# Where the embedding gathers of a DLRM tower are issued: one paced by single waits, one in bursts

## What is computed

```python
e = stack([tbl_f[ids[:, f]] for f in range(26)], axis=1)      # 2048 x 26 x 128
T = concatenate([r_dense[:, None, :], e], axis=1)             # 2048 x 27 x 128
Z = einsum('bnd,bmd->bnm', T, T)
h = concatenate([Z[:, iu0, iu1], r_dense], axis=1)            # 351 + 128 columns
h = maximum(h @ W_top1 + b_top1, 0)                           # 512
h = maximum(h @ W_top2 + b_top2, 0)                           # 256
y = h @ W_top3                                                # 2048 x 1
```

## Time and profile before

| what | us |
|---|---|
| median of 3 runs | 453.94 |
| lowest, highest | 452.58, 459.67 |
| the profiled execution | 448.83 |
| its span | 447.0 |
| TensorE busy (matmul) | 388.3 (87%) |
| VectorE busy | 262.2 (59%) |
| ScalarE busy | 156.7 (35%) |
| GpSimd busy | 235.8 (53%) |
| mean granted TensorE clock, share of 2.4 GHz | 0.950 |

### The profile page before, as it was taken

How to read it: one execution, slowest core, us unless ns; L and a number is a source line. 1 busy time by engine, 2 the same in 40 slices (tenths; PEclk the granted TensorE clock), 3 DMA queues, 4 the chain that set the end, 5 groups by cost and what they waited for, 6 DMA issues and landing times.

```text
span 447.0 us, 9767 instructions
## 1 busy us (share of the span) xinstructions
PE 388.3 (87%) x4139; PEld 353.5 (79%) x4139; DVE 262.2 (59%) x440; ACT 156.7 (35%) x215; POOL 235.8 (53%) x252
## 2 busy tenths in 40 slices
PE   7678487798988999889997999889997999898997
PEld 5568487687868889779887989779886889787897
DVE  4369558677736764666846674586845674572131
ACT  5236424251441615215351414325251424315321
POOL 6658555545655546645565456555565546556000
PEclk9869978998999999989999899999999999899899
DMA  8974211345231521234121531235121431242230
GB/s 210 252 213 125 56 47 45 96 99 166 55 85 41 140 73 41 72 90 125 37 85 42 121 92 41 84 70 148 39 67 48 105 109 48 54 108 75 41 52 18
DMA packets 48393, 39.26 MB, mean 88 GB/s; under 512 B 33073, under 2 KB 42592, under 8 KB 48350
## 3 DMA queue, kind: packets, MB, share of 16 engines
q1 hardware_dynamic: 38913, 22.38, 19.4%
q0 software_dynamic: 7808, 16.01, 14.1%
q10 hardware_dynamic: 1628, 0.25, 0.4%
HBM read 32.59 MB, written 6.03 MB: 86 GB/s over the span
## 4 chain that ended last, share of the span: by engine, by line
PE 78%; issue 10%; DVE 5%; another core or an unknown queue 3%; ACT 3%; DVEq 0%; ACTq 0%
PE look_ps L896 34%; PE gram_ps L928 15%; PE mlp_ps L948 9%; PE look_ps L906 6%; PE mlp_ps L958 5%; DVE hot L574 4%; PE look_ps L887 3%; ACT T L752 1%; ACT T L744 1%; PE look_ps L1000 1%; ACT tab_hi L719 1%; PE look_ps L970 1%; PE look_ps L992 1%; DVE hot L579 1%
## 5 line engine op out<-in xcount | busy, mean ns | idle before, releaser
L536 POOL DMA_INDIRECT rows<-in_tbl_dram,ids_all x228 | 219.2, 961 | 168.7 <-PE look_ps L896 58.3
L574 DVE TENSOR_TENSOR hot<-ids_near,gram_ps 125x2048 fp32r<-125x2048 f16 x60 | 135.7, 2285 | 77.0 <-PE look_ps L896 68.5
L896 PE MATMUL look_ps<-hot,tab_hi 125*128 125x256 f32 x664 | 172.2, 297 | 9.3 <-issue 4.2
L896 PE MATMUL look_ps<-hot,tab_lo 125*128 125x256 f32 x664 | 166.8, 289 | 0.0
L896 PEld LDWEIGHTS look_ps<-hot,tab_hi 125*128 125x128 f32 x664 | 131.5, 198 | 13.6 <-issue 7.5
L896 PEld LDWEIGHTS look_ps<-hot,tab_lo 125*128 125x128 f32 x664 | 131.7, 198 | 0.1
L744 ACT COPY T<-look_ps 128x512 f32<-128x512 f32 x38 | 45.4, 1196 | 205.2 <-PE look_ps L896 76.9
L928 PE MATMUL gram_ps<-T 128*54 128x54 f32 x2048 | 78.0, 222 | 37.3 <-issue 29.6
L928 PEld LDWEIGHTS gram_ps<-T 128*54 128x54 f32 x2048 | 66.3, 136 | 50.9 <-issue 43.0
L752 ACT COPY T<-look_ps 128x384 f32<-128x384 f32 (+2 forms) x80 | 75.7, 1050 | 34.3 <-PE look_ps L906 19.8
L606 DVE COPY gram<-gram_ps 128x486 f32<-128x486 f32 (+1 forms) x64 | 37.9, 606 | 40.4 <-remote 30.0
(11 more groups left out here) (81 smaller groups left out, 162.6 us busy)
## 6 DMA issues: line engine op xcount, KB each, us to landing
dots<-gram SPq DMA_DIRECT2D x28, 182.2 KB
ids_near<-ids_rows SPq DMA_DIRECT2D x25, 192.0 KB
rows<-in_tbl_dram,ids_all POOLq DMA_INDIRECT x228
T<-in_tbl_dram SPq DMA_DIRECT2D x4, 448.0 KB
pairs<-dots SPq DMA_DIRECT2D x14, 117.0 KB
gram<-in_tbl_dram SPq DMA_DIRECT2D x3, 448.0 KB
rows<-in_r_dense_dram SPq DMA_DIRECT2D x16, 64.0 KB
w<-in_tbl_dram SPq DMA_DIRECT2D x2, 448.0 KB
```

The source lines that it names most:

```text
L536: pool.indirect_dma_start(rows[:, t % 2, place[n], :], None, tables[n - 1], bass.IndirectOffsetOnAxis(ap=index[:, n - 1:n].bitcast(U32), a ...
L574: eq = nc.vector.tensor_tensor(hot[:VP, count % 2], near, steps[:VP].rearrange("p (c q) -> p c q", q=1).to_broadcast([VP, CH, Q]), ALU.is_ ...
L896: mm = pe.matmul(dst, w[:VP, k, c], hot[:VP, slot, c], start=(c == 0 and half == 0), stop=(c == CH - 1 and half == 1))
```

## The change

It replaces the single waits by a few: for tiles 0 to 3 EARLY names the gathers that wait, and for what. For the others BURSTS (and BURSTS_END in unit 6) says which of a unit's 30 gathers wait for which step; all others follow without a wait for pace. The waits for `turned` in gather stay. In steady state the bursts have 7, 6, 3, 5, 6 and 3 gathers.

```diff
-            STEP_MORE = (4, 5, 6, 6, 8, 8, 8, 10, 10, 11, 12, 12, 13, 13, 15, 16, 16, 17, 18, 19, 20, 21, 21, 22, 23, 23, 24, 25, 26, 26, 27, 28)
-            STEP_LESS = (4, 5, 6, 6, 8, 8, 8, 10, 10, 11, 12, 12, 13, 15, 16, 16, 17, 18, 19, 20, 21, 21, 22, 23, 24, 25, 26, 27, 28, 29)
+
+            EARLY = ({7: (hot_looked, 1), 12: (hot_looked, 3)},
+                     {0: (hot_looked, 5), 5: (hot_looked, 6), 10: (hot_looked, 9)},
+                     {0: (gram_done, 1), 6: (turned, 8), 11: (hot_looked, 14)},
+                     {0: (gram_done, 5), 6: (hot_looked, 17), 11: (turned, 15)})
+
+            BURSTS = {0: 5, 7: 11, 13: 16, 16: 20, 21: 24, 27: 27}
+            BURSTS_END = {0: 5, 7: 11, 13: 15, 16: 16, 21: 19, 27: 21}
...
             def keep_pace(t, i):
 
-                if t == 0:
-                    if i == 14:
-                        pool.wait_ge(hot_looked, 2)
-                elif t == 1:
-                    if i in (1, 4, 8, 12, 14):
-                        pool.wait_ge(hot_looked, {1: 2, 4: 4, 8: 6, 12: 8, 14: 9}[i])
-                elif t == 2:
-                    if i == 4:
-                        pool.wait_ge(gram_done, 3)
-                    elif i in (1, 8, 12, 15):
-                        pool.wait_ge(hot_looked, {1: 10, 8: 12, 12: 14, 15: 16}[i])
-                elif t == 3:
-                    if i in (1, 12):
-                        pool.wait_ge(gram_done, 6 if i == 1 else 10)
-                    elif i in (4, 8, 15):
-                        pool.wait_ge(hot_looked, {4: 17, 8: 19, 15: 22}[i])
-                elif i not in (0, 3, 7, 11, 14 if t // 2 < ADDED else 13):
-                    u = t // 2 - 1
+                if t < len(EARLY):
+                    if i in EARLY[t]:
+                        pool.wait_ge(*EARLY[t][i])
+                    return
+                u, at = t // 2 - 1, 15 * (t % 2) + i
+                bursts = BURSTS if u + 1 < END else BURSTS_END
+                if at in bursts:
                     steps_u = progress(u) + (progress(u + 1) if u + 1 < END else [])
-                    pool.wait_ge(*steps_u[min((STEP_MORE[16 * (t % 2) + i] if u + 1 < ADDED else STEP_LESS[15 * (t % 2) + i]),
-                                          len(steps_u) - 1)])
+                    pool.wait_ge(*steps_u[bursts[at]])
```

## The result

Median of three runs 488.33 us (486.87 to 491.37) against 453.94 before; ratio 1.0785, 95% interval 1.0659 to 1.0911. The change costs 34 us where a gain of 19 was forecast. The profiled execution took 491.37 us, its span is 489.6 against 447.0.

A forecast was written before the change was run, and what follows sets the result against it. TensorE was taken to bound the kernel, its dots slowed beside GpSimd's gathers. Steady units -13.2, unit 6 -3, start -4, VectorE +1 sum to -19.2 us against 453.94: 434.7 us, range 414 to 456.

The forecast's parts named there:

- The second halves: Second dots halves of tiles 0 and 1 in a unit: 3.62 and 4.17 us, each to keep 0.3 us over 1.96.
- the dots of tile 14: Dots after unit 6: 7.90 us against 3.49 undisturbed; last gathers now end before them, 4.2 us gained.
- not the cause: Rival: gathers only lie beside the slow dots, or the overlap merely shifts; 448 to 456 us, centre 452, chance 0.22.
- Tile 0's first half: First dots half of a unit, 1.65 us before: two gathers would lie inside, costing 1.6 us, between 0 and 2.47.
- the row with two inside: Profile row of tile 1's first dots half at 181.09: two gathers start inside, 4.12 us, 2.47 over the undisturbed 1.65.
- Tile 1's first half: Third dots half of a unit, 4.12 us before: one gather inside after five others, costing 1.5 us, between 0 and 2.47.
- The clock: Granted clock in the dots stretches: 1.00 in all but one (0.91 at 409.08), so held not to be the cause.
- The first 100 us: Tiles 0 to 3, with 11 waits in place of 16: 4 us gained; bounds a gain of 7.7 + 5.2, a loss of 2 x 2.47.
- VectorE's wait: Idle time of VectorE before 22.79 in the start: 7.71 us, to shrink to 1 to 3.
- Unit 6: Unit with its own burst list: first halves lose 1.6, gain 1.4, the pile adds 1, tile 14 gains 4.2; together 3 us gained.
- The pile of eight gathers: Bursts of 3 and 5 in or behind tile 13's four dots pieces in unit 6: 1 us added, between -2 and +4.
- The slower rival: Burst of six across tile 0's first half, three or more gathers starting inside: a unit loses 2.47 us, 475 us, chance 0.09.

The follow-up runs named there:

- steady_only_b: Kernel before with only the bursts for tiles 4 to 13, old waits elsewhere: 452.45 us against 448.77 for before.
- early_only_b: Kernel before with only the new waits for tiles 0 to 3, old pace from tile 4 on: 463.45 us against 448.77 for before.
- end_only_b: Kernel before with only the bursts for tiles 14 and 15 (BURSTS_END), old waits elsewhere: 453.53 us against 448.77 for before.
- earlier_bursts: Kernel before with bursts from tile 4 on that begin earlier than the change's, old waits for tiles 0 to 3: 374.73 us against 373.33 for before.

## Why the prediction was wrong

It read the cause rightly and set its sizes wrongly, nearly all in one direction.

- **Right.** The gathers beside the dots are the cause (46.1 us for those of tiles 4 to 15 on a held chip). The second halves went to 1.94 us (2.0 to 2.3 forecast), the dots of tile 14 from 7.90 to 3.73, a gain of 4.2 as written. The rival "not the cause" falls on held chips.
- **Tile 0's first half: taken at 1.6 over, bounded by 2.47.** It cost 3.6 to 4.3 in units 2 to 5 (5.3 to 6.0 us against 1.65). This is the step that failed in the steady part. The prediction placed the burst rightly, two of its gathers in the half and one just ahead, but priced it by how many gathers start inside, and below the row with two inside, which had cost 2.47. It also held the other measure, the pause that lasts to about a microsecond after the last gather. By it, a burst that ends 2.9 us into the half holds it until 3.9 us, and with the records that are left it takes some 4.6, above the bound of 1.65 + 2.47. The remaining 1.3 us to the measured 5.86 could not be read from before: the hold lasted 1.7 us after a run of six, and the last records ran at half clock.
- **Tile 1's first half: taken at 1.5 over.** It was 3.3 in most units (4.9 against 1.6) by the same fault. The burst also began later than placed (358.38 is 11.8 us after the second half's end, not 10.6), so that two gathers started inside and not one. With it the four halves cost 3.9 + 0 + 3.3 + 0 = 7.2 us over the undisturbed, where before they cost 6.3: the gathers were moved from two halves into the two others. So the dots account for 1 us of loss a unit instead of a gain of 2.6.
- **The clock, left out.** The prediction saw full clock in five of six stretches of dots and wrote the clock off; it did not look at what runs behind them. This is the other 2 us of a unit's 3.1. At 3.4 us of half speed a unit takes 51.5 to 51.9 us before and 52.4 after; at 10.2 us, which before has in none of these units, it takes 54.4 to 54.9. The same bursts in steady_only_b had 10.2 us in one unit of five and lost 3.7 us in all; what decides between the two is not known.
- **The first 100 us: a gain of 4, it was a loss of 13.1.** The prediction named new bursts that start inside the dots and priced them at 2.47 a tile at worst; with six gathers inside tile 0's dots cost 5.8 us more, and with nine inside, three of them the end of a run of ten that it did not see, tile 1's cost 8.4. VectorE's wait shrank as forecast (7.71 to 1.71 us), but it brought nothing: first dots at 56.9 us, 56.5 before. early_only_b (+14.7) confirms this part alone.
- **Unit 6: 3 us gained, with the gain of 4.2 in it.** Unit 6 and what follows cost 13.9 us instead. The pile of eight gathers behind the first two pieces was priced at 1 us with 4 as its end; the dots took 12.2 us for 7.8 and the three lookups 20.6 for 11.4. end_only_b alone cost 4.8 us, so part of this was not there without the rest of the change.
- **The slower rival** (475 us, 0.09) had the mechanism and its deciding point, three or more gathers in tile 0's first half, which the trace of after shows at the edge (two start inside, one 0.6 us ahead). It lacked the clock and the start, the difference to 488. Its chance was set too low: the burst's 7.5 us in a gap of 4.3, which stood in the prediction, already put a run's end inside the half.

Open: why a chip is held or free; whether requests made by GpSimd need a DMA at all to hold TensorE; why the same bursts leave 3.4 us at half speed in one unit and 10.2 in the next; whether earlier_bursts gains on a held chip, as it was not seen on one. The Trainium skill ("DMA: Bandwidth & Descriptors", "Terms") says that GpSimd writes these descriptors to rings in SBUF; that they meet TensorE's reads there is a guess that no run here tested. No version was found that beats the kernel before: on a held chip all that do the whole work were slower, on a free one they lie within 0.6% (the whole change was not run there).

## What to carry to other kernels

Price an overlap by where the other engine's run ends in the stage and by how long that run is, not by how many of its instructions fall inside; and don't start a run at a signal that is given inside the stage to be protected. After a hold, look at the granted clock of what follows. When waits are moved, follow each run of the other engine to its end: a run of ten gathers that the prediction had not placed let only 8 records through in 5.5 us. And measure the kernel before on the same chip: here the same code takes 374 or 450 us, and the parts of this change cost 0.8 to 2.9% on the one kind and at most 0.6% on the other.

## What was not expected of the hardware

- Two kinds of chip: the kernel before takes 373 to 374 us on four of seven and 449 to 456 on three. With gathers of tiles 4 to 15 left out the gap narrows to 372.95 against 402.65; in what is left of it the gathers of tiles 0 to 3 still run, and the first dots begin at 40.9 us on the one, 53.2 on the other.
- On a held chip gathers one after another every 1.25 us stop 54-column matmuls until 0.6 us (two gathers) to 1.7 us (six) after the last; with an eighth of the bytes it is much the same (1.2 to 1.5 us after six).
- Signals come late and together after a run of gathers: VectorE waited until 433.83 for pieces of dots, 1.9 us after the eighth gather's end.
- Holds of 3 to 4 us, twice in a unit, go with 10.2 us of half clock in some units and with 3.4 us in others, a difference of 2 to 3 us in the unit's length.
